# Two dense sample groups instead of one, sums by accumulated transposes, six gathered groups in the first five expert steps

## The reference

```python
h = layernorm(x)                                   # layer 0, deformable convolution
v = (h @ v_w + v_b).reshape(b, h, w, G, C)         # G = 8 groups of C = 32 channels
deform = (h @ qd_w + qd_b + prior) * sigmoid(h @ qs_w + dscale) * 6.0   # K = 9 points (x, y) a group
weights = h @ qw_w + qw_b
# bilinear sample of v at each of the 72 points: 4 corners, zero outside the image
samp = g(y0,x0)*wy0*wx0 + g(y0,x0+1)*wy0*wx1 + g(y0+1,x0)*wy1*wx0 + g(y0+1,x0+1)*wy1*wx1
x = x + einsum('bhwgkc,bhwgk->bhwgc', samp, weights).reshape(.., 256) @ out_w + out_b
x = x + experts_0(layernorm(x))                    # top-1 of 8 experts, 128 -> 512 -> 128
x = x + neighbourhood_attention(layernorm(x))      # 7x7 window, 8 heads
x = x + experts_1(layernorm(x))
```

## Time and profile before

| | us |
|---|---|
| median of 3 runs (lowest, highest) | 3019.55 (3014.43, 3028.98) |
| the profiled execution, its own time | 3027.92 |
| its span | 3025.8 |
| PE busy | 2254.1 (74%) |
| DVE busy | 2084.3 (69%) |
| ACT busy | 1094.1 (36%) |
| POOL busy | 2175.3 (72%) |
| mean granted TensorE clock | 0.853 of full |

### The profile page before, as it was taken

One profiled execution on the slowest core, in us unless ns is written; L12 is line 12 of the kernel. 1 busy time (PEld: TensorE's weight loads), 2 busy tenths in 40 slices (PEclk: granted clock), 3 DMA queues, 4 the chain that ended last, 5 costly groups with the idle time before them and its releaser, 6 DMA issues.

```text
span 3025.8 us, 54249 instructions
## 1 busy us (share of the span) xinstructions
PE 2254.1 (74%) x16544; PEld 2134.3 (71%) x16544; DVE 2084.3 (69%) x4371; ACT 1094.1 (36%) x3526; POOL 2175.3 (72%) x2085
## 2 busy tenths in 40 slices
PE   1355667787877777887787878778787877777788
PEld 0354657777777777787777778777777777777777
DVE  4556657677767677876677777767677766777643
ACT  1012224333434343343343334334343433443355
POOL 2777777777777777777777777777777777777700
PEclk6677778898988889898888888988888988888899
DMA  9511212222212222221222222122111111111100
GB/s 185 129 53 53 60 49 61 61 61 61 60 54 54 60 61 60 62 61 54 56 61 61 61 61 60 53 55 60 57 54 54 53 55 49 54 54 54 55 15 10
DMA packets 262111, 181.03 MB, mean 60 GB/s; under 512 B 187923, under 2 KB 224805, under 8 KB 262021
## 3 DMA queue, kind: packets, MB, share of 16 engines
q0 software_dynamic: 64512, 132.25, 14.3%
q1 hardware_dynamic: 197508, 47.77, 7.5%
HBM read 157.48 MB, written 22.37 MB: 59 GB/s over the span
## 4 chain that ended last, share of the span: by engine, by line
POOL 58%; issue 21%; PE 10%; DVE 6%; SPq 3%; DMA 1%; ACT 1%; POOLq 1%; DVEq 0%; ACTq 0%
POOL got L751 57%; PE Y L1422 3%; PE Z L1413 2%; PE N L1326 1%; SPq L635 1%; DVE got L967 1%; DVE acc L1042 1%; DVE summed L970 1%; SPq L614 1%; DMA got<-patches,ranks 1%; PE N L1480 1%; PE N L1488 1%; POOL ranks L743 1%; DVE made L890 1%; ACT hid L1239 0%
## 5 line engine op out<-in xcount | busy, mean ns | idle before, releaser
L751 POOL DMA_INDIRECT got<-patches,ranks x2016 | 2152.6, 1068 | 652.5 <-issue 592.5
L1422 PE MATMUL Y<-w,hid 128*128 128x128 f32 x4096 | 653.9, 311 | 577.2 <-DVE acc L1042 492.2
L1422 PEld LDWEIGHTS Y<-w,hid 128*128 128x128 f32 x4096 | 584.6, 220 | 611.0 <-DVE acc L1042 379.1
L1239 ACT ACTIVATE hid<-Z,b 128x128 f32<-128x128 f32 x2048 | 576.6, 369 | 641.2 <-PE Z L1413 640.2
L1326 PE MATMUL N<-ident,made 128*128 128x128 f32 x4608 | 577.4, 286 | 76.7 <-issue 43.9
L1326 PEld LDWEIGHTS N<-ident,made 128*128 128x128 f32 x4608 | 557.6, 201 | 95.3 <-issue 58.8
L1413 PE MATMUL Z<-xt_m,w 128*128 128x128 f32 x4096 | 586.0, 293 | 0.5 <-ACT xt_m L1221 0.5
L1413 PEld LDWEIGHTS Z<-xt_m,w 128*128 128x128 f32 x4096 | 545.9, 208 | 13.3 <-issue 7.2
L970 DVE TENSOR_REDUCE summed<-got 128x32 f32<-128x1152 f32 x224 | 475.4, 2122 | 7.7
L967 DVE TENSOR_TENSOR got<-got,wq 128x1152 f32<-128x1152 f32 x224 | 303.0, 1353 | 159.1 <-DMA got<-patches,ranks 159.0
L890 DVE TENSOR_TENSOR made<-tent 128x1024 f32<-128x1024 f32 x288 | 341.3, 1220 | 9.6 <-PE N L1326 8.1
(11 more groups left out here) (204 smaller groups left out, 2260.8 us busy)
## 6 DMA issues: line engine op xcount, KB each, us to landing
got<-patches,ranks POOLq DMA_INDIRECT x2016, 2.4
vwin<-vpad SPq DMA_DIRECT2D x320, 40.0 KB
patches<-arena SPq DMA_DIRECT2D x92, 128.0 KB
patches<-got SPq DMA_DIRECT2D x38, 128.0 KB, 3.6
w<-in_L_ffn_w SPq DMA_DIRECT2D x2, 2048.0 KB
vpad<-vt SPq DMA_DIRECT2D x128, 16.0 KB
out<-X SPq DMA_DIRECT2D x32, 64.0 KB, 1.8
X<-in_x SPq DMA_DIRECT2D x1, 576.0 KB, 4.5
```

The costliest lines, as they stand in the source:

```text
L751: pool.indirect_dma_start(out=got[:, q, j * PATCH:(j + 1) * PATCH], out_offset=None, in_=table, in_offset=bass.IndirectOffsetOnAxis(ap=ran ...
L1239: ins = a.activation(hid[:, e % 2, c, :], Z[e % 2][:, c * P:(c + 1) * P], ACT.Relu, bias=b1[n][:, e * FC + c:e * FC + c + 1])
L1422: ins = pe.matmul(Y[:, (e % 4) * D:(e % 4 + 1) * D], hid[:, e % 2, c, :], w2[n][:, e * FC + c, :], start=(c == 0), stop=(c == FC - 1))
```

## The change

Groups 6 and 7 become dense, so that `DG` = 6 groups stay gathered: 54 gathers a tile and a table of 6 groups an image. There are 18 dense points instead of 9. They use the banks N one group after the other: nine sums, `copyA`, `lookA`, nine sums, `copyB`, `lookB`.

The sums on PE are written as transposes that accumulate (`is_transpose=True`). The gathered groups are summed in this way too: DVE only multiplies, and PE adds the nine transposed 128x128 blocks of a group (4 corners x 32 channels) into a new bank S. ACT copies S out in two halves (before group 3 may start, and after group 5), and the projection multiplies each group's 128 rows with a four times repeated `out_w`. Only the 64 dense channels are still transposed by themselves. `places` computes corners for 54 points.

```diff
-DG = G - 1
+DG = G - 2
...
-        OT = sb("OT", [P, NH, P])[:, :, :]
+        OT = PT
...
+        S = bank("S")
...
                     if e == 0:
...
+                        dense("make", i, range(4, 6))
+                        dense("sum", i, range(2, 4))
                     if e == 1:
...
-                        dense("make", i, range(0, 2))
+                        dense("make", i, range(6, 8))
+                        dense("sum", i, range(4, 6))
...
                     if e == 7:
                         if ends:
                             route("share", 0, i - 1)
-                        conv(1, i)
-                        dense("look", i)
+                        dense("sum", i, range(16, 18))
+                        dense("copyB", i)
 
                 def beside_first(e):
                     if e == 0:
+                        dense("lookB", i)
...
-                        conv(2, i)
+                        conv(0, i)
+                        conv(1, i)
                     if e == 1:
...
-                        conv(3, i)
+                        conv(2, i)
...
                     if e == 4:
                         if att:
                             attend("values", i - 3)
-                        if final:
-                            conv(6, i)
+                        conv(5, i)
+                        if tents:
+                            dense("apart", i + 1)
...
                     if e == 6:
...
+                            dense("make", i + 1, range(0, 2))
...
                     if e == 7:
...
-                        if not final:
-                            conv(6, i)
                         if tents:
-                            dense("weigh", i + 1)
+                            dense("make", i + 1, range(2, 4))
+                            dense("sum", i + 1, range(0, 2), i - 3 if att else None)
...
                     v.tensor_tensor(g3, g3, wj.unsqueeze(2).to_broadcast([P, QJ * CORNERS, C]), ALU.mult)\
                         .then_inc(*s(f"m{q}"))
-                    v.wait_ge(*d(f"m{q}", t))
-                    v.tensor_reduce(summed[:, q * C:(q + 1) * C],
-                                    got[:, q, :].rearrange("p (j c) -> p c j", c=C), AX.X, ALU.add)\
-                        .then_inc(*s(f"r{q}"))
...
-                    v.wait_ge(*dense_t.done("look", looked))
+                    v.wait_ge(*dense_t.done("lookB", looked))
...
+                if part == HALF - 1:
+                    a.wait_ge(*conv_t.done(f"g{HALF - 1}", t))
+                    a.wait_ge(*dense_t.done("lookB", t))
+                    a.wait_ge(*conv_t.done("proj", t - 1))
+                    a.activation(sums[:, 0:half_sums + DC], S[:, 0:half_sums + DC], ACT.Copy)\
+                        .then_inc(*conv_s.step("half0"))
...
                             ins = pe.matmul(N[c // 4][:, (c % 4) * P:(c % 4 + 1) * P],
                                             made[:, k % MADE, c * P:(c + 1) * P], ident[:, :],
-                                            start=(k == 0 and c % 4 == 0), stop=(k == K - 1 and c % 4 == 3))
+                                            start=(k % K == 0 and c % 4 == 0), stop=(k % K == K - 1 and c % 4 == 3),
+                                            is_transpose=True)
...
+                if isinstance(part, int):
+                    q = part
+                    pe.wait_ge(*conv_v.done(f"m{q}", t))
+                    if q % HALF == 0:
+                        pe.wait_ge(*(conv_s.done("half1", t - 1) if q == 0 else conv_s.done("half0", t)))
+                    for j in range(QJ):
+                        ins = pe.matmul(S[:, (q % HALF) * P:(q % HALF + 1) * P],
+                                        got[:, q, j * PATCH:(j + 1) * PATCH], ident[:, :],
+                                        start=(j == 0), stop=(j == QJ - 1), is_transpose=True)
+                    ins.then_inc(*s(f"g{q}"))
...
-                            pool.wait_ge(*conv_v.done(f"r{q}", t - 1))
+                            pool.wait_ge(*conv_t.done(f"g{q}", t - 1))
```

More of the change, by code:

```diff
@@ L271, in build @@
         place_t = Steps(sem("place_t"), "xT offs")
-        dense_v = Steps(sem("dense_v"), "apart weigh m0 m1 m2 m3 m4 m5 m6 m7 m8")
-        dense_s = Steps(sem("dense_s"), "abs tent s0 s1 out")
-        dense_t = Steps(sem("dense_t"), "k0 k1 k2 k3 k4 k5 k6 k7 k8 look")
+        ks = range(KD)
+        dense_v = Steps(sem("dense_v"), "apart weigh " + " ".join(f"m{k}" for k in ks))
+        dense_s = Steps(sem("dense_s"), "abs tent sA0 sA1 sB0 sB1")
+        dense_t = Steps(sem("dense_t"), " ".join(f"k{k}" for k in ks[:K]) + " k9 k10 lookA " +
+                        " ".join(f"k{k}" for k in ks[K + 2:]) + " lookB")
         ts = range(LEAD)
@@ L339, in beside_second @@
                             route("share", 1, i - 4)
-                        dense("sum", i, range(0, 2), i - 4 if att else None)
-                        dense("make", i, range(2, 4))
+                        dense("make", i, range(8, 10))
+                        dense("sum", i, range(6, 8))
                     if e == 3:
@@ L373, in beside_second @@
                             route("gate_T", 0, i - 1)
-                        conv(0, i)
-                        dense("sum", i, range(7, 9))
-                        dense("copy", i)
+                        dense("make", i, range(16, 18))
+                        dense("sum", i, range(14, 16))
                     if e == 7:
@@ L418, in beside_first @@
                             route("stats", 1, i - 3)
+                        if tents:
+                            dense("weigh", i + 1)
                         if final:
@@ L944, in _ @@
             dense("weigh", 0)
+            dense("make", 0, range(0, 4))
             v.wait_ge(const_in, CONSTS)
@@ L1356, in _ @@
                     places(part, t, (LEAD - 1, -1))
+            dense("sum", 0, range(0, 2))
             pe.wait_ge(setup, 7 + NH)
```

182 lines of the change are left out of this document (100 added, 82 removed).

## The result

| | before | after |
|---|---|---|
| median, us (lowest, highest) | 3020.28 (3014.43, 3028.98) | 3197.99 (3196.97, 3199.95) |
| profiled span, us | 3025.8 | 3195.5 |
| mean granted TensorE clock | 0.853 | 0.896 |
| PE busy, DVE busy, POOL busy, us | 2254, 2084, 2175 | 2517, 1914, 1895 |

The change makes the kernel slower, by a ratio of 1.0587 (95% interval 1.056 to 1.0613). That is 178 us, where 71 were forecast.

The account below looks back on a forecast made before the run. POOL's gathers bound the kernel at 88.2 us a slot, a DVE and PE loop close behind. Legs of 43.2, 28.1 and 18.9 plus 2 x 1.15 gave 92.5; +120 in 28 slots, -49 filling: 3091 us, range 2940 to 3260.

Parts of the forecast that it names:

- The second bound of the kernel before: A loop where DVE and PE wait for each other, some 85.5 us a slot if gathers came at once.
- second layer's leg: Part of the DVE and PE loop between DVE's additions, second layer: 43.8 us before, 43.2 forecast after.
- first layer's steps 0 to 4: Leg to the end of the fourth addition, where PE becomes the long side: 28.1 us instead of 24.2.
- the rest of it: Remaining first-layer leg, from PE's down through projection, makes and routing: 18.9 us at full clock.
- half clock in these two: Two half-clocked stretches partly on PE's path, outside the second layer's leg: 2 x 1.15 us a slot.
- about +1.4 in two waits: End of second layer's leg: last down waits for PE's 16 more transposes, about 1.4 us more.
- My upper end of 96.5 us a slot: Loop if each of three 2 us waits brings 3.5 us at half clock: 96.5 us a slot.
- the filling: Slots 0 to 3, where DVE waits for gathers: 12.25 us saved each, -49 us in all.
- the full clock: Rival: PE stays at full clock, loop 89 to 90.3 us, total 2993 to 3030 us; chance 0.17.
- the full clock doesn't engage for transposes: Rival on PE: transposes don't hold the clock; 3600 us, or 3350 if in a quarter; chance 0.11.
- The factor of four for fp32: Rival on PE: transposes at a quarter save 3.4 us a slot, total 3000 us; chance 0.03.
- The faster side: Rival: early multiplies let DVE run ahead, waits overlap, gathers stay the bound; 2853 or 2628 us; chance 0.15.

Follow-up runs that it names:

- a_warm2: Kernel after plus small needless matmuls on constants, sized to PE's waits before groups 2, 4, 5, the queries and the second layer's down(4): 3047.5 us.
- a_red: Kernel after with DVE again summing each gathered group's nine points and PE doing one transpose per group instead of nine: 3526.4 us, ratio 1.168.
- a_mul_q_pl: Kernel after with multiplies earlier in DVE's order, queries written into tile PT, and `places` moved to step 4 of the first layer's run: 2777.4 us, ratio 0.9218.
- best_w: a_mul_q_pl plus small matmuls in PE's waits before the second layer's down(0) and down(4): 2744.7 us, ratio 0.9088 to the kernel before.
- a_mm: Kernel after with the dense groups' sums by plain fp32 matmuls instead of transposes: 3597.0 us, ratio 1.1922 to the kernel before.
- a_mul: Kernel after with each of DVE's multiplies one or more places earlier in its order, PE's order unchanged: 2955.7 us, ratio 0.9791 to the kernel before.
- b_tr: Kernel before with its one dense group's sums as accumulated transposes: 3032.5 us, ratio 1.0049.
- a_one: Kernel after with one of the nine transposes of each gathered group, the other eight points left out: 3121.3 us, ratio 1.0349 to the kernel before.

## Why the prediction was partly wrong

Right was which loop takes over. The gathers left the path, POOL stands 17 us a slot (15 forecast) waiting for PE's sums, and DVE's queries wait 4.4 us (3 forecast). PE waits 1.82 to 2.05 us at groups 2, 4 and 5 (2.0). Transposes are single instructions of 0.113 us. The drain has kept its length. The direction held, and the time lies just inside the forecast's own range (3030 to 3203), but at less than half the true size of the loss. The second bound of the kernel before, "some 85.5 us", is 85.3; the sum that I gave for it, 88.2 less half of 159 over 25 slots, gives 85.0.

The slot was forecast as "90.2 plus 2 x 1.15 = 92.5". The sentence on what holds half clock already ("as measured") fits only the first leg of that list, the second layer's: it alone was taken from a measured length, the other two were added up from prices at full clock. So the terms are set beside the runs in this way:

| term, us a slot | forecast | measured |
|---|---|---|
| second layer's leg, its half clock included | 43.2 | 45.3 |
| first layer's steps 0 to 4, at full clock | 28.1 | 28.7 |
| the rest of it, at full clock | 18.9 | 18.9 |
| half clock in these two | 2.3 | 2.6 |
| slot | 92.5 | 95.57 |

The full-clock values are from `a_warm2`. The two stretches at 1.15 each are there (1.0 behind group 2, 1.65 behind group 5), so that term was nearly right.

The step that failed is the second layer's leg, 43.2, and in it "about +1.4 in two waits". I had taken the leg of before with its half clock as it was and added 1.4 for DVE's waits for PE. These waits were 7.1 us in that leg before (1.03 and 2.30 below, and the 3.80 of the earlier trace rows) and are 10.1 now, in eight waits, so they grew by 3.0.

```profile
1568.73 0.17 DVE L1017 TENSOR_TENSOR route<-M,taken 128x8 f32<-128x8 f32 x1 [1.03 <-PE M L1394]
...
1590.44 0.17 DVE L1001 TENSOR_TENSOR route<-CV,gb 128x8 f32<-128x8 f32 x1 [2.30 <-PE CV L1388]
```

In `a_warm2`, the same work at full clock, they are 6.0 us, and the leg is 40.9 instead of 45.3. So 4.4 us of the leg are half clock: 1.63 up to DVE's addition of the projection, and 2.78 behind the wait of 6.30 us, where a chain of PE's work (down, dense sums, look) lies on the path. For that place I had priced 16 more transposes at full clock. The leg of before held two such stretches as well:

```profile
1564.80:1571.20 6.40, 5.24 (x25) 5.24 (x26) 3.33 (x15) 0.55 (x2) 4.88 (x6) 0.50 0.17 53
1588.30:1591.60 3.30, 3.30 (x17) 3.30 (x18) 1.02 (x7) 0.91 (x4) 2.69 (x3) 0.51 0.20 60
```

What they cost there no run shows, so how much of the 2.1 us is more half clock and how much is work that I had wrong stays open. My upper end of 96.5 us a slot is near the truth by luck: it adds half clock behind the waits of the first layer's legs, and the excess came in the other leg.

The difference of 98.7 us between the forecast's span (+71) and the profile's (+169.7) splits so: 19 x 3.07 = 58 from these slots, 41 of it from the second layer's leg. 6 x 6.45 = 39 from the second loop's, which I had not priced apart. 14 from the filling, where I took 49 and it was 35.3 up to the second query row (at 429.98, against 465.26). The last slots give 12 back.

In the second loop's slots DVE closes the first layer's run late: its four additions come in two parts, with idle times of 0.84 to 1.14 and 1.05 to 1.33 us before them that the trace calls issue, 2.2 us a slot. PE waits 3.9 to 4.2 us for them instead of 1.86.

```profile
2487.44 1.12 DVE L1064 SCALAR_TENSOR_TENSOR acc<-Y,route,acc 128x128 f32<-128x128 f32 x3 [0.93 <-issue]
2489.62 0.35 DVE L1064 SCALAR_TENSOR_TENSOR acc<-Y,route,acc 128x128 f32<-128x128 f32 x1 [1.05 <-issue]
```

`a_warm2` has the same waits and slots of 92.9 us on the mean, 3.8 above its others, so this is not mainly the clock. The kernel before has one such wait of 0.75 to 0.92 us a slot there, and its second loop's slots are 0.4 us longer than the first's. The three runs that have none in the second loop, `a_red`, `a_mul_q_pl` and `best_w`, have slots 1.0 to 4.6 us shorter there than in the first (the last two have these waits in the first). So these waits go with the longer slots. Why DVE waits there was not tried.

Of the rivals, the full clock is refuted for this kernel as written (0.896) and, forced, gives 3047.5 us, where I had 2993 to 3030: the leg sum was near, the filling and the second loop were not. Part 4 (PE-mode transpose) of the Trainium skill's TensorE: Matmul & The Clock Gate says that the full clock doesn't engage for transposes. In `a_warm2` 198 transposes a slot, among 710 PE instructions, ran at a granted clock of 1.00; no run has long stretches of transposes alone. The factor of four for fp32 that the Terms of the same page of the Trainium skill give the transposing mode was two here, by the pitch of single rows and by `a_mm`. The faster side did not occur, but it lay only an order of DVE's instructions away (`a_mul`, 0.9791).

## What to carry to other kernels

Price a wait of PE twice: the wait, and what PE has to do behind it on the path at half clock. Here that was another 1.0 to 2.8 us behind four waits of six and nothing behind two. Do it in the leg taken from a measured length too, since there the waits change as well. Where PE falls to half clock in each turn of a loop, test an edit by measuring, since 0.7 us can cost 3.4 and a second gain can be worth a quarter of what it was alone.

When sums move from DVE to PE in an order fixed by hand, move what feeds them too. The same instructions, with each multiply placed ahead of the work that it had stood behind, turned 5.9% slower into 2.1% faster.

## What the hardware showed that I had not expected

Idle work made the kernel faster: 3648 needless matmul instructions gave 150 us (`a_warm2`). Less work on PE lowered its clock: 0.853 to 0.826 in `b_tr`, 0.896 to 0.871 in `a_one`. A small matmul of 64 columns cost as much as a transpose of 128: 52 instructions in 5.92 us, 0.11 each. And in ten kernels whose slots hold stretches at half clock the slots' lengths lay 3.41 us apart or a few times that (85.32, 88.75, 92.16, 95.57, 98.99, 109.23).
